# A new order of steps and PSUM banks in a two-attention, eight-expert layer

## The chip, the cores and the metric

One core of a Trainium2 chip runs the kernel. The metric is device microseconds of one execution. A core has TensorE (matmuls and transposes, with a weight load before each), VectorE, ScalarE, GpSimd, and SyncE, which only issues transfers. Each works through its own instructions in order and waits on semaphores. TensorE writes into eight PSUM banks; a bank holds 128 partitions of 512 floats.

## The reference, cut to what matters

```python
def _attn(q_in, k_in, v_in, wq, bq, wk, bk, wv, bv, wo, bo, causal):
    Q = (q_in @ wq + bq).reshape(Bq, Sq, H, HD)       # H = 16 heads of HD = 8
    Kp = (k_in @ wk + bk).reshape(Bq, Sk, H, HD)
    V = (v_in @ wv + bv).reshape(Bq, Sk, H, HD)
    scores = einsum('bqhd,bkhd->bhqk', Q, Kp) / sqrt(HD)     # causal mask in the first
    return einsum('bhqk,bkhd->bqhd', softmax(scores), V).reshape(Bq, Sq, Dm) @ wo + bo

def _moe(x, rw, rb, w1, b1, w2, b2):                  # E = 8 experts, K = 2 of them per token
    router_weights = softmax(xf @ rw + rb)
    topw, topi = top_k(router_weights, K);  topw = softmax(topw)
    h = gelu(einsum('td,edf->etf', xf, w1) + b1)      # D = 128, F = 512
    eo = einsum('etf,efd->etd', h, w2) + b2
    return einsum('etd,te->td', eo, combine)

x = _layernorm(x + _attn(x, x, x, ..., True), ln1_g, ln1_b)
x = _layernorm(x + _attn(x, ctx, ctx, ..., False), ln2_g, ln2_b)
x = _layernorm(x + _moe(x, ...), ln3_g, ln3_b)
```

x is 16 sequences of 128 tokens of 128 floats, the context 16 sequences of 77 tokens. All in float32.

## The kernel before, in words

The 16 sequences are worked on in eight pairs, p = 0 to 7. Each pair goes through self-attention (`SA`), cross-attention (`CA`) and routing (`RT`). Each of these is cut into named steps: `turn` (transpose the input), `project` and `project_keys`, `spread_terms` and `spread_keys` (lay the 16 heads out over the partitions), `values`, `scores` in four parts, `shift` (the negative row maxima, transposed and added to the queries as extra rows), `weights` in four parts (scores again and exp), `mix` in four parts (weights times values), `restore` in four parts (transpose back and divide), `turn_heads` and `norm` (output projection, residual, layer norm). Parts 0 and 1 are of sequence u = 0 of the pair, parts 2 and 3 of u = 1. In `scores` and `weights` a part covers two groups of heads, one in each of the two banks that the step has.

Two copies are made by transfers: `spread_keys` writes ku by VectorE, and SyncE copies it into km, from which `scores` reads; `spread_terms` writes qu by ScalarE, and SyncE copies it into qm. Both are issued at u = 1 (lines 469 and 482).

Routing: `route` (transpose and logits; ScalarE copies r_xT between them), `gate`, `choose`, `second` (two top-1 searches of small VectorE operations), `place` (rank in each expert's region by matmul), `number` (row numbers, then GpSimd's four indirect transfers of the pair's token rows into the DRAM array `dispatched`, line 1259). Before a pair's rows are sent, its share of `dispatched` has to be filled with a neutral row: `fill`, two transfers by SyncE (line 455). Each waits for the dispatch of the pair before it (line 452), and `number` waits for the fill (line 1253).

Experts (`MOE`): 39 tiles of 128 rows, `slots`. The first 17 can be settled after pair 5 (`count`, `table`), the rest after pair 7. `rows` n loads tile n from `dispatched` (line 511), `slot_turn` transposes it and VectorE copies it and the expert's first-layer weights into place (lines 1156, 1157), `slot_hidden` does the first layer and gelu, `slot_output` the second layer, and GpSimd scatters the result (line 1264). The weights of both layers, 2 MB each, lie where SA's large buffers were, so `first_layer` (line 498) waits for SA's last scores and `second_layer` (line 503) for its last weights. The first load waits for the table and for pair 5's dispatch:

```python
    if n == 0:
        sp.wait_ge(s_table, EARLY_OPS)
        sp.wait_ge(r.s_disp, KNOWN * 4 * 16)
        sp.wait_ge(SA.s_u_ps, PAIRS * 4)
        sp.wait_ge(SA.s_t_ps, PAIRS * 4)
```

and VectorE's first `slot_turn` waits for the first layer's weights (line 1150, `dve.wait_ge(s_w1, 16)`).

The order of all steps is one list written out. `ORDER` holds (kind, step, part, ahead); `iteration(i)` runs it with pair i + ahead, for i = -1 to 6, and each engine takes from it the steps in which it has work, in that order. Then `FINAL`, with explicit pairs, does what is left. So the order on each engine is the list, filtered: a step moved in the list moves on all engines that have a part in it, and on no other.

`home` gives each step its bank or banks; `last_home` holds for pair 7. On TensorE, `take(b)` waits until the last user of bank b has been read out, which is what `give(b, semaphore, value)` noted. A step that takes a bank right behind another waits for the engine that reads that bank.

After the tail of slots, the results are loaded back in four parts, summed, normed and stored.

## Time and profile before

| | us |
|---|---|
| median of the timed runs (463.62 to 465.36) | 464.87 |
| the profiled execution | 461.8 |
| its span | 460.1 |

The page begins with the busy time of each engine. A timeline row says when an instruction started (us from the span's start), how long it took, engine, line, what it wrote and read, and in brackets how long the engine was idle before it and what ended that. `bank` is PSUM; sa_, ca_ and r_ are tiles of the two attentions and the router. PEld is TensorE's weight load, SPq SyncE's queue; there the length is the time of issuing, not of the transfer. sa_over_km and sa_over_qm are the two layers' weights, sa_pt<-dispatched a load of expert rows. The granted clock is the share of full speed that TensorE had.

### The profile page before, as it was taken

The numbers are of one execution on the slowest core, as the hardware profiler recorded it, in microseconds if no ns is written. First come the engines' busy times: TensorE is split into PE (matmuls) and PEld (weight loads), VectorE is DVE, ScalarE is ACT, GpSimd is POOL, SyncE is SP. The second block draws the span as 40 slices with busy tenths as digits, with TensorE's granted clock in tenths as the row PEclk, the third lists the DMA queues.
The fourth block names the chain that finished last, engine by engine and source line by source line (L and its number), as shares of the span: only waits on it lengthen the run. The fifth ranks groups of instructions, "written<-read, shape, count | busy, mean of one in ns | idle before, by whom it ended". The sixth has DMA issues, their size and how long they took to land.

```text
span 460.1 us, 8844 instructions
## 1 busy us (share of the span) xinstructions
PE 367.9 (80%) x2122; PEld 245.3 (53%) x2122; DVE 310.2 (67%) x1075; ACT 293.0 (64%) x664; POOL 162.0 (35%) x212
## 2 busy tenths in 40 slices
PE   4388689988998998998988998889788578999600
PEld 2235355554564554645545545438656467999500
DVE  6153545678777787777877888876665774556366
ACT  4047249769768867967866966786795733555314
POOL 8312122132243144142253234241225254455522
PEclk9999879999999999999999999899999979999955
DMA  8700330621342333225036044682504113220063
GB/s 209 216 0 1 88 73 1 175 55 25 83 145 54 71 108 99 51 82 147 11 94 168 6 93 138 177 249 65 162 24 147 29 40 90 59 63 29 14 182 91
DMA packets 36073, 41.59 MB, mean 90 GB/s; under 512 B 4794, under 2 KB 28207, under 8 KB 36024
## 3 DMA queue, kind: packets, MB, share of 16 engines
q1 hardware_dynamic: 33752, 36.79, 30.4%
q0 software_dynamic: 2272, 4.24, 2.9%
q8 instruction: 20, 0.33, 0.3%
q14 instruction: 29, 0.24, 0.2%
HBM read 13.66 MB, written 14.79 MB: 62 GB/s over the span
## 4 chain that ended last, share of the span: by engine, by line
PE 49%; DVE 22%; issue 9%; ACT 8%; DMA 5%; POOL 4%; SPq 2%; DVEq 1%; POOLq 0%; ACTq 0%
PE bank L666 8%; PE bank L761 8%; PE bank L748 7%; PE bank L653 4%; ACT sa_qm L831 4%; DMA sa_km<-sa_ku 3%; PE bank L598 3%; PE bank L634 3%; DVE ca_nm L971 3%; PE bank L599 3%; PE bank L633 3%; PE bank L677 3%; POOL dispatched L1259 2%; SPq L469 2%; PE bank L641 1%
## 5 line engine op out<-in xcount | busy, mean ns | idle before, releaser
L890 ACT ACTIVATE sa_us<-bank,expert_b 128x128 f32<-128x128 f32 x156 | 44.4, 368 | 36.7 <-PE bank L748 30.9
L1236 POOL TENSOR_SCALAR_AFFINE_SELECT sa_pt<-sa_pt 128x512 f32<-128x512 f32 x64 | 39.0, 636 | 70.2 <-ACT sa_pt L839 69.9
L1264 POOL DMA_INDIRECT results<-sa_us,sa_pt x39 | 41.0, 1050 | 59.8 <-DVE sa_us L1169 44.6
L971 DVE TENSOR_REDUCE sa_nm<-bank 128x4 f32<-128x512 f32 x64 | 41.7, 685 | 18.9 <-PE bank L634 18.7
L761 PE MATMUL bank<-sa_over_qm,sa_us 128*128 x312 | 44.7, 289 | 5.7 <-DVE yb L1167 3.2
L831 ACT CAST sa_qm<-bank 8x512 fp32r<-8x512 f32 x64 | 36.8, 575 | 15.4 <-PE bank L641 14.1
L761 PEld LDWEIGHTS bank<-sa_over_qm,sa_us 128*128 128x128 f32 x312 | 39.8, 200 | 9.1 <-issue 8.9
L748 PE MATMUL bank<-xsT,sa_pt 128*128 128x128 f32 x312 | 43.2, 283 | 1.3 <-DVE sa_pt L1157 1.0
L839 ACT ACTIVATE sa_pt<-bank 128x512 f32<-128x512 f32 x64 | 34.8, 596 | 11.6 <-PE bank L653 11.5
L748 PEld LDWEIGHTS bank<-xsT,sa_pt 128*128 128x128 f32 x312 | 38.7, 195 | 4.2 <-DVE xsT L1156 2.2
L831 ACT CAST ca_qm<-bank 8x512 fp32r<-8x512 f32 x64 | 36.8, 575 | 5.2 <-PE bank L641 4.0
L634 PE MATMUL bank<-sa_km,sa_qu 128*128 128x512 f32 x64 | 39.4, 669 | 0.0
L1259 POOL DMA_INDIRECT dispatched<-r_sent,r_row x32 | 31.4, 981 | 21.2 <-issue 10.5
L839 ACT ACTIVATE ca_pt<-bank 77x512 f32<-77x512 f32 x64 | 33.8, 597 | 6.6 <-PE bank L653 6.6
L633 PE MATMUL bank<-causal_bf,ident_bf 128*128 128x512 bf16 x64 | 28.3, 442 | 11.9 <-DMA sa_km<-sa_ku 11.3
L666 PE MATMUL bank<-ca_pt,ca_vo 77*64 77x512 f32 x128 | 34.9, 617 | 1.1 <-DVE ca_lk L931 0.6
L666 PE MATMUL bank<-sa_pt,sa_vo 128*64 128x512 f32 x128 | 35.2, 632 | 0.0
L1244 POOL TENSOR_TENSOR sa_rs<-sa_ba,half 128x1 f32<-128x1 f32 x16 | 10.2, 634 | 68.4 <-DVE sa_ba L1015 68.4
L971 DVE TENSOR_REDUCE ca_nm<-bank 128x4 f32<-128x308 f32 x64 | 27.3, 472 | 7.3 <-PE bank L634 6.8
L653 PE MATMUL bank<-sa_qm,sa_ku 128*128 128x512 f32 x64 | 26.1, 482 | 5.7 <-ACT ca_qu L820 3.5
L846 ACT COPY ca_us<-bank 128x512 f32<-128x512 f32 x32 | 18.6, 589 | 15.0 <-PE bank L666 14.9
L633 PEld LDWEIGHTS bank<-causal_bf,ident_bf 128*128 128x128 bf16 x64 | 6.7, 105 | 36.7 <-DMA sa_km<-sa_ku 16.8
(218 smaller groups left out, 845.9 us busy)
## 6 DMA issues: line engine op xcount, KB each, us to landing
dispatched<-filler SPq DMA_DIRECT2D x17, 520.0 KB, 4.7
sa_km<-sa_ku SPq DMA_DIRECT2D x32, 128.0 KB, 2.4
sa_qm<-sa_qu SPq DMA_DIRECT2D x32, 96.0 KB
ca_qm<-ca_qu SPq DMA_DIRECT2D x32, 96.0 KB
sa_pt<-dispatched SPq DMA_DIRECT2D x39, 65.0 KB, 2.1
ca_km<-ca_ku SPq DMA_DIRECT2D x32, 77.0 KB, 2.1
sa_over_km<-in_e_w SPq DMA_DIRECT2D x1, 2048.0 KB, 9.1
sa_pt<-results SPq DMA_DIRECT2D x8, 256.0 KB, 4.8
```

The lines of the kernel that those rows point to most:

```text
L633: pe.matmul(dst, ident_bf[:, :], causal_bf[:, :].rearrange("q (o n) -> q o n", o=1).to_broadcast([P, J, P]), start=True, stop=False)
L634: pe.matmul(dst, k.qu[:, g, P * u:P * u + P], k.km[:, :, (2 * g + u) * k.keys:(2 * g + u) * k.keys + k.kpad], start=not k.causal, stop=Tru ...
L653: pe.matmul(bank[b][0:k.keys, :], k.ku[:, g, k.keys * u:k.keys * u + k.keys], k.qm[:, :, g, P * u:P * u + P], start=True, stop=True).then_ ...
L666: ins = pe.matmul(bank[b][64 * (g % 2):64 * (g % 2) + 64, :], k.vo[:, u, g, :], k.pt[u][:, 512 * g:512 * g + 512], start=True, stop=True)
L748: ins = pe.matmul(bank[b][:, P * (c if n < EARLY else c % 2):][:, 0:P], w1_now[n % 2][:, P * c:P * c + P], xsT[n % 2][:, :], start=True, s ...
L761: ins = pe.matmul(bank[b][:, 0:D], hid[n % 2][:, c, :], w2[:, bass.ds(expert, 1), c, :].rearrange("f o d -> f (o d)"), start=(c == 0), sto ...
L831: act.copy(k.qm[rows, j, :, P * u:P * u + P], src).then_inc(k.s_sha, 1)
L839: act.activation(k.pt[u][:, 512 * g:512 * g + 512], bank[home_of(p)[k, "weights", u][g % 2]][0:k.keys, :], ACT.Exp, scale=SCALE).then_inc( ...
L890: act.activation(hid[n % 2][:, c, :], bank[b][:, P * (c if n < EARLY else c % 2):][:, 0:P], ACT.Gelu, bias=b1[:, bass.ds(expert * FC + c, ...
L971: dve.tensor_reduce(k.nm[:, u, g, :], bank[home_of(p)[k, "scores", u][g % 2]][:, :].rearrange("q (j n) -> q j n", j=J)[:, :, 0:k.keys], AX ...
L1259: pool.indirect_dma_start(out=dispatched, out_offset=bass.IndirectOffsetOnAxis(ap=r.row[:, v, c:c + 1], axis=0), in_=r.sent[:, v, c, :], i ...
L1264: pool.indirect_dma_start(out=results, out_offset=bass.IndirectOffsetOnAxis(ap=xs[n % RING][:, P:P + 1].bitcast(I32), axis=0), in_=ys[n % ...
```

## The change

Only the three tables change: `ORDER` and `FINAL`, and the banks in `home` and `last_home`. Every engine does the same steps with the same operations as before. The head of `ORDER` is cut at another point (CA restore 2 and 3, project and project_keys now open the iteration), and within it steps trade places. `fill` was (RT, "fill", 0, -1) near the end, in front of (CA, "fetch", 0, 1); it is now (RT, "fill", 0, -2) near the head. SyncE takes part in SA turn, fetch, fill and the spread steps alone. In `FINAL`, `first_layer` comes behind rows 0, 1 and 2; before, it came in front of `second_layer` and all rows.

```diff
         ORDER = [
-            (SA, "scores", 2, 0), (CA, "turn_heads", 1, -2), (CA, "spread_terms", 0, -1), (CA, "spread_keys", 0, -1),
-            (CA, "spread_keys", 1, -1), (CA, "spread_terms", 1, -1), (CA, "norm", 1, -2), (SA, "weights", 0, 0),
-            (SA, "scores", 3, 0), (SA, "weights", 1, 0), (CA, "values", 0, -1), (RT, "route", 0, -2),
-            (RT, "gate", 0, -2), (SA, "mix", 0, 0), (SA, "shift", 1, 0), (CA, "scores", 0, -1),
-            (RT, "choose", 0, -2), (SA, "restore", 0, 0), (SA, "mix", 1, 0), (CA, "scores", 1, -1),
-            (SA, "weights", 2, 0), (CA, "scores", 2, -1), (SA, "turn", 0, 1), (SA, "weights", 3, 0),
-            (CA, "shift", 0, -1), (RT, "second", 0, -2), (CA, "scores", 3, -1), (SA, "restore", 1, 0),
-            (SA, "project", 0, 1), (SA, "project_keys", 0, 1), (SA, "mix", 2, 0), (CA, "weights", 0, -1),
-            (SA, "mix", 3, 0), (SA, "turn_heads", 0, 0), (CA, "shift", 1, -1), (RT, "place", 0, -2),
-            (SA, "spread_terms", 0, 1), (SA, "spread_keys", 0, 1), (SA, "restore", 2, 0), (SA, "spread_keys", 1, 1),
-            (SA, "spread_terms", 1, 1), (SA, "restore", 3, 0), (SA, "norm", 0, 0), (SA, "values", 0, 1),
-            (CA, "mix", 0, -1), (SA, "turn_heads", 1, 0), (CA, "weights", 1, -1), (SA, "norm", 1, 0),
-            (CA, "weights", 2, -1), (RT, "number", 0, -2), (CA, "restore", 0, -1), (CA, "mix", 1, -1),
-            (SA, "scores", 0, 1), (CA, "weights", 3, -1), (CA, "restore", 1, -1), (CA, "mix", 2, -1),
-            (SA, "scores", 1, 1), (CA, "turn_heads", 0, -1), (CA, "turn", 0, 0), (CA, "turn_context", 0, 0),
-            (RT, "fill", 0, -1), (CA, "mix", 3, -1), (SA, "shift", 0, 1), (CA, "norm", 0, -1),
-            (CA, "restore", 2, -1), (CA, "restore", 3, -1), (CA, "project", 0, 0), (CA, "project_keys", 0, 0),
-            (CA, "fetch", 0, 1)]
+            (CA, "restore", 2, -2), (SA, "values", 0, 0), (CA, "restore", 3, -2), (CA, "project", 0, -1),
+            (CA, "project_keys", 0, -1), (SA, "scores", 2, 0), (CA, "turn_heads", 1, -2), (RT, "fill", 0, -2),
+            (CA, "spread_terms", 0, -1), (CA, "spread_keys", 0, -1), (CA, "spread_keys", 1, -1),
+            (CA, "spread_terms", 1, -1), (CA, "norm", 1, -2), (SA, "weights", 0, 0), (SA, "scores", 3, 0),
+            (SA, "weights", 1, 0), (RT, "route", 0, -2), (SA, "mix", 0, 0), (RT, "gate", 0, -2), (SA, "shift", 1, 0),
+            (RT, "choose", 0, -2), (CA, "values", 0, -1), (SA, "restore", 0, 0), (SA, "mix", 1, 0),
+            (CA, "scores", 0, -1), (SA, "weights", 2, 0), (CA, "scores", 1, -1), (SA, "turn", 0, 1),
+            (SA, "weights", 3, 0), (CA, "shift", 0, -1), (RT, "second", 0, -2), (CA, "scores", 2, -1),
+            (SA, "restore", 1, 0), (SA, "mix", 2, 0), (CA, "scores", 3, -1), (SA, "project", 0, 1),
+            (SA, "project_keys", 0, 1), (CA, "weights", 0, -1), (SA, "turn_heads", 0, 0), (SA, "mix", 3, 0),
+            (SA, "spread_terms", 0, 1), (CA, "shift", 1, -1), (RT, "place", 0, -2), (SA, "spread_keys", 0, 1),
+            (SA, "spread_keys", 1, 1), (SA, "spread_terms", 1, 1), (SA, "restore", 2, 0), (SA, "restore", 3, 0),
+            (SA, "norm", 0, 0), (CA, "mix", 0, -1), (SA, "turn_heads", 1, 0), (CA, "weights", 1, -1),
+            (SA, "norm", 1, 0), (CA, "weights", 2, -1), (CA, "fetch", 0, 1), (RT, "number", 0, -2),
+            (CA, "mix", 1, -1), (CA, "mix", 2, -1), (CA, "restore", 0, -1), (SA, "scores", 0, 1),
+            (CA, "weights", 3, -1), (CA, "restore", 1, -1), (SA, "scores", 1, 1), (CA, "turn", 0, 0),
+            (CA, "turn_heads", 0, -1), (CA, "mix", 3, -1), (CA, "turn_context", 0, 0), (SA, "shift", 0, 1),
+            (CA, "norm", 0, -1)]
...
         home = {
-            (CA, "mix", 0): (6, 3), (CA, "mix", 1): (5, 2), (CA, "norm", 0): (5,), (CA, "norm", 1): (1,),
-            (CA, "project", 0): (0,), (CA, "project_keys", 0): (3,), (CA, "scores", 0): (2, 3),
-            (CA, "scores", 1): (6, 0), (CA, "shift", 0): (3,), (CA, "shift", 1): (7,), (CA, "spread_keys", 0): (6,),
-            (CA, "spread_keys", 1): (0,), (CA, "spread_terms", 0): (4,), (CA, "spread_terms", 1): (3,),
-            (CA, "turn", 0): (6,), (CA, "turn_context", 0): (7,), (CA, "turn_heads", 0): (4,),
-            (CA, "turn_heads", 1): (5,), (CA, "values", 0): (4,), (CA, "weights", 0): (3, 0),
-            (CA, "weights", 1): (7, 4), (RT, "place", 0): (2,), (RT, "route", 0): (5, 1), (SA, "mix", 0): (0, 1),
-            (SA, "mix", 1): (5, 4), (SA, "norm", 0): (1,), (SA, "norm", 1): (1,), (SA, "project", 0): (2,),
-            (SA, "project_keys", 0): (7,), (SA, "scores", 0): (0, 1), (SA, "scores", 1): (1, 7),
-            (SA, "shift", 0): (4,), (SA, "shift", 1): (5,), (SA, "spread_keys", 0): (1,),
-            (SA, "spread_keys", 1): (6,), (SA, "spread_terms", 0): (3,), (SA, "spread_terms", 1): (0,),
-            (SA, "turn", 0): (5,), (SA, "turn_heads", 0): (6,), (SA, "turn_heads", 1): (4,), (SA, "values", 0): (5,),
-            (SA, "weights", 0): (3, 2), (SA, "weights", 1): (4, 7)}
+            (CA, "mix", 0): (6, 3), (CA, "mix", 1): (5, 1), (CA, "norm", 0): (1,), (CA, "norm", 1): (5,),
+            (CA, "project", 0): (0,), (CA, "project_keys", 0): (3,), (CA, "scores", 0): (5, 2),
+            (CA, "scores", 1): (4, 0), (CA, "shift", 0): (3,), (CA, "shift", 1): (7,), (CA, "spread_keys", 0): (2,),
+            (CA, "spread_keys", 1): (7,), (CA, "spread_terms", 0): (4,), (CA, "spread_terms", 1): (4,),
+            (CA, "turn", 0): (5,), (CA, "turn_context", 0): (3,), (CA, "turn_heads", 0): (4,),
+            (CA, "turn_heads", 1): (1,), (CA, "values", 0): (1,), (CA, "weights", 0): (3, 5),
+            (CA, "weights", 1): (1, 6), (RT, "place", 0): (2,), (RT, "route", 0): (1, 4), (SA, "mix", 0): (2, 7),
+            (SA, "mix", 1): (5, 4), (SA, "norm", 0): (0,), (SA, "norm", 1): (7,), (SA, "project", 0): (1,),
+            (SA, "project_keys", 0): (6,), (SA, "scores", 0): (2, 0), (SA, "scores", 1): (5, 6),
+            (SA, "shift", 0): (7,), (SA, "shift", 1): (6,), (SA, "spread_keys", 0): (0,),
+            (SA, "spread_keys", 1): (6,), (SA, "spread_terms", 0): (3,), (SA, "spread_terms", 1): (1,),
+            (SA, "turn", 0): (7,), (SA, "turn_heads", 0): (2,), (SA, "turn_heads", 1): (4,), (SA, "values", 0): (4,),
+            (SA, "weights", 0): (3, 0), (SA, "weights", 1): (4, 1)}
...
         FINAL = [
...
-            (SA, "shift", 1, 7), (RT, "second", 0, 5), (SA, "restore", 0, 7), (MOE, "first_layer", 0, 0),
-            (CA, "scores", 0, 6), (CA, "turn_context", 0, 7), (CA, "scores", 1, 6), (MOE, "second_layer", 0, 0),
...
-            (SA, "turn_heads", 0, 7), (CA, "weights", 0, 6), (CA, "shift", 1, 6), (MOE, "table", 0, 0),
-            (CA, "mix", 0, 6), (SA, "restore", 2, 7), (MOE, "rows", 0, 0), (SA, "restore", 3, 7),
-            (CA, "weights", 1, 6), (SA, "norm", 0, 7), (SA, "turn_heads", 1, 7), (CA, "project_keys", 0, 7),
-            (MOE, "rows", 0, 1), (CA, "restore", 0, 6), (SA, "norm", 1, 7), (MOE, "rows", 0, 2),
-            (CA, "weights", 2, 6), (MOE, "rows", 0, 3), (MOE, "rows", 0, 4), (CA, "mix", 1, 6),
-            (CA, "weights", 3, 6), (CA, "mix", 2, 6), (CA, "turn", 0, 7), (CA, "restore", 1, 6), (MOE, "rows", 0, 5),
-            (CA, "spread_keys", 0, 7), (CA, "spread_keys", 1, 7), (MOE, "slot_turn", 0, 0), (CA, "turn_heads", 0, 6),
-            (CA, "project", 0, 7), (CA, "norm", 0, 6), (CA, "mix", 3, 6), (MOE, "slot_hidden", 0, 0),
-            (MOE, "slot_turn", 0, 1), (CA, "values", 0, 7), (CA, "restore", 2, 6), (CA, "restore", 3, 6),
-            (MOE, "slot_turn", 0, 2), (MOE, "slot_hidden", 0, 1), (MOE, "slot_output", 0, 0),
...
+            (SA, "weights", 3, 7), (CA, "shift", 0, 6), (RT, "number", 0, 5), (CA, "scores", 2, 6),
+            (SA, "mix", 2, 7), (CA, "scores", 3, 6), (CA, "weights", 0, 6), (MOE, "count", 0, 0), (SA, "mix", 3, 7),
+            (CA, "shift", 1, 6), (SA, "turn_heads", 0, 7), (MOE, "table", 0, 0), (SA, "restore", 2, 7),
+            (CA, "mix", 0, 6), (MOE, "second_layer", 0, 0), (SA, "restore", 3, 7), (MOE, "rows", 0, 0),
+            (CA, "weights", 1, 6), (CA, "restore", 0, 6), (SA, "turn_heads", 1, 7), (CA, "project_keys", 0, 7),
+            (CA, "weights", 2, 6), (SA, "norm", 0, 7), (SA, "norm", 1, 7), (MOE, "rows", 0, 1), (MOE, "rows", 0, 2),
+            (MOE, "first_layer", 0, 0), (CA, "mix", 1, 6), (MOE, "rows", 0, 3), (CA, "mix", 2, 6),
+            (CA, "weights", 3, 6), (CA, "spread_keys", 0, 7), (CA, "restore", 1, 6), (CA, "turn", 0, 7),
+            (CA, "spread_keys", 1, 7), (MOE, "slot_turn", 0, 0), (CA, "project", 0, 7), (CA, "restore", 2, 6),
+            (CA, "mix", 3, 6), (MOE, "slot_turn", 0, 1), (CA, "turn_heads", 0, 6), (MOE, "rows", 0, 4),
+            (MOE, "slot_hidden", 0, 0), (CA, "norm", 0, 6), (CA, "spread_terms", 0, 7), (MOE, "slot_turn", 0, 2),
+            (MOE, "slot_hidden", 0, 1), (CA, "restore", 3, 6), (MOE, "slot_output", 0, 0), (MOE, "rows", 0, 5),
...
```

The lines of `FINAL` left out interleave the steps of pairs 6 and 7 with slots 0 to 16 in nearly the order of before, and `last_home` gets other banks throughout.

## Rows read from the trace of the kernel before

**Rows 1.** The page: busy time of each engine, its share of the span, instructions.
```profile
PE 367.9 (80%) x2122; PEld 245.3 (53%) x2122; DVE 310.2 (67%) x1075; ACT 293.0 (64%) x664; POOL 162.0 (35%) x212
```

**Rows 2.** Windows of three stages: length, PE, PEld, DVE, ACT, POOL busy, clock, DMA, GB/s.
```profile
171.70:208.60 36.90, 33.49 (x184) 19.86 (x182) 28.83 (x102) 28.19 (x59) 12.63 (x20) 1.00 0.35 94
284.20:360.00 75.80, 62.88 (x385) 42.83 (x385) 53.54 (x210) 55.62 (x124) 26.60 (x36) 0.98 0.46 131
360.00:431.00 71.00, 61.97 (x489) 58.16 (x488) 43.11 (x157) 37.63 (x120) 33.59 (x32) 0.95 0.18 50
```

**Rows 3.** Timeline, TensorE, one iteration: start, length, ..., [idle before, released by].
```profile
172.42 0.70 PE L653 MATMUL bank<-sa_qm,sa_ku 128*128 128x512 f32 x2 [0.55 <-ACT ca_qu L820]
175.71 0.61 PE L706 MATMUL bank<-router_w,r_xT 128*128 128x8 f32 x4 [0.49 <-ACT r_xT L858]
183.45 0.33 PE L641 MATMUL bank<-cst,ca_mm 128*128 128x128 f32 x1 [1.00 <-DVE ca_mm L981]
199.71 0.39 PE L633 MATMUL bank<-causal_bf,ident_bf 128*128 128x512 bf16 x1 [0.41 <-DVE sa_nm L971]
203.31 1.09 PE L677 MATMUL bank<-cst,ca_us 128*128 128x128 f32 x8 [0.38 <-DVE ca_y L1009]
206.38 0.39 PE L598 MATMUL bank<-ca_hq,spread_hq 128*128 128x256 f32 x1 [0.25 <-DVE ca_lq L931]
```

**Rows 4.** Timeline, SyncE's queue, the same iteration.
```profile
205.17 0.94 SPq L455 DMA_DIRECT2D dispatched<-filler  x2
206.15 1.07 SPq L428 DMA_DIRECT2D ca_cin<-in_ctx  x1
208.63 2.46 SPq L469 DMA_DIRECT2D ca_km<-ca_ku  x4
```

**Rows 5.** The page's DMA issues: bytes of one, median us from issue to landing.
```profile
dispatched<-filler SPq DMA_DIRECT2D x17, 520.0 KB, 4.7
sa_over_km<-in_e_w SPq DMA_DIRECT2D x1, 2048.0 KB, 9.1
```

**Rows 6.** A source line, timeline rows of the same iteration, two groups of the page.
```profile
L962 DVE TENSOR_TENSOR sa_vo<-bank,sa_rows x8: 416/417/426, 14.2 to 267.9; 128x256 f32<-128x256 f32 x8
...
183.32 0.16 DVE L1071 SCALAR_TENSOR_TENSOR r_by_expert<-r_by_expert 128x16 f32<-128x16 f32 x1
185.07 0.16 DVE L1076 TENSOR_TENSOR r_by_token<-r_by_token 128x2 f32<-128x2 f32 x1
...
196.29 0.10 PEld L633 LDWEIGHTS bank<-causal_bf,ident_bf 128*128 128x128 bf16 x1 [0.81 <-DMA sa_km<-sa_ku]
...
L971 DVE TENSOR_REDUCE ca_nm<-bank 128x4 f32<-128x308 f32 x64 | 27.3, 472 | 7.3 <-PE bank L634 6.8
L846 ACT COPY ca_us<-bank 128x512 f32<-128x512 f32 x32 | 18.6, 589 | 15.0 <-PE bank L666 14.9
```

**Rows 7.** Timeline, SyncE's queue, at the first expert tile.
```profile
292.37 0.52 SPq L498 DMA_DIRECT2D sa_over_km<-in_e_w  x1
296.23 0.82 SPq L503 DMA_DIRECT2D sa_over_qm<-in_e_w  x1
310.19 6.32 SPq L511 DMA_DIRECT2D sa_pt<-dispatched  x6
```

**Rows 8.** Timeline, GpSimd's dispatch of pair 5, and landing of all 32 such transfers.
```profile
302.51 0.96 POOL L1259 DMA_INDIRECT dispatched<-r_sent,r_row  x1 [0.31 <-issue]
...
DMA to landing us min/median/max: 2.3/2.3/7.2
```

**Rows 9.** Windows of 2 us around the weight loads, columns as in rows 2.
```profile
292.00:294.00 2.00, 2.00 (x6) 0.91 (x7) 1.79 (x7) 1.35 (x3) 0.40 (x1) 0.56 0.60 135
296.00:298.00 2.00, 2.00 (x13) 0.99 (x11) 1.79 (x7) 1.98 (x4) 1.22 (x2) 1.00 1.03 393
306.00:308.00 2.00, 1.48 (x11) 1.00 (x10) 1.40 (x6) 1.37 (x4) 1.05 (x2) 1.00 0.92 283
```

**Rows 10.** Timeline, VectorE's copy in the first slot_turn.
```profile
313.54 0.29 DVE L1156 COPY xsT<-bank 128x128 f32<-128x128 f32 x1 [0.52 <-issue]
```

More of the change, by code:

```diff
@@ L378, in build @@
-        last_home = {**home,
-            (CA, "mix", 0): (5, 2), (CA, "mix", 1): (5, 1), (CA, "norm", 0): (2,), (CA, "norm", 1): (1,),
-            (CA, "scores", 0): (5, 6), (CA, "scores", 1): (1, 0), (CA, "shift", 0): (2,), (CA, "shift", 1): (4,),
-            (CA, "spread_keys", 0): (2,), (CA, "spread_keys", 1): (7,), (CA, "spread_terms", 0): (2,),
-            (CA, "spread_terms", 1): (2,), (CA, "turn_heads", 0): (6,), (CA, "turn_heads", 1): (1,),
-            (CA, "values", 0): (1,), (CA, "weights", 0): (6, 7), (CA, "weights", 1): (3, 1), (RT, "place", 0): (6,),
-            (RT, "route", 0): (4, 5)}
+            (CA, "restore", 2, -2), (SA, "values", 0, 0), (CA, "restore", 3, -2), (CA, "project", 0, -1),
@@ new lines, in build @@
+        last_home = {**home,
+            (CA, "mix", 0): (0, 2), (CA, "mix", 1): (1, 5), (CA, "norm", 0): (2,), (CA, "norm", 1): (3,),
+            (CA, "scores", 0): (6, 5), (CA, "scores", 1): (7, 0), (CA, "shift", 0): (1,), (CA, "shift", 1): (5,),
+            (CA, "spread_keys", 0): (2,), (CA, "spread_keys", 1): (2,), (CA, "spread_terms", 0): (2,),
+            (CA, "spread_terms", 1): (4,), (CA, "turn_heads", 0): (3,), (CA, "turn_heads", 1): (0,),
+            (CA, "values", 0): (3,), (CA, "weights", 0): (1, 4), (CA, "weights", 1): (3, 5), (RT, "place", 0): (5,),
+            (RT, "route", 0): (0, 2)}
```

67 lines of the change are left out of this document (34 added, 33 removed).

## The prediction

> **What bounds the kernel now.** I read the page's busy shares first: TensorE 80%, VectorE 67%, ScalarE 64% [rows 1]. An average over stages with different limits says little, so the next view was the busy time by stage [rows 2]. In a steady iteration (36.9 us from one to the next; five of them, pairs 2 to 6) TensorE is busy 33.5 us, VectorE 28.8, ScalarE 28.2: TensorE bounds it, and a new order can at most give back the time in which TensorE waits. In the last attention part and the first expert tiles (284 to 360 us) TensorE has 62.9 of 75.8 us, in the rest of the expert tiles 62.0 of 71 [rows 2]. So three views follow: TensorE's own rows with their waits in one iteration, SyncE's queue there, and the same two around the first expert tile.
>
> TensorE's rows that have idle time in front of them in one iteration are six: 0.55, 0.49, 1.00, 0.41, 0.38 and 0.25 us, together 3.08 us [rows 3]. That is the most that the change can win per iteration, 15.4 us over five. SyncE waits for the dispatch of the pair before, issues the two fills at 205.17, the context load at 206.15 and the km copies of CA at 208.63 [rows 4]. None of the six waits names a DMA.
>
> **The filler.** From the two lists, SyncE's program before is: SA copies, fill, fetch, then CA copies. After it is: SA copies, fetch, fill, then CA copies. `fill` moves to the head of the next iteration with its pair lowered by one, so it is the same fill, with the same wait for the same dispatch. Only the 77 KB context load steps in front of it. It was needed some 30 us later (the turn of the context follows in the next iteration), so it wins nothing: 0 us. The CA copies still stand behind the filler: the chain and TensorE's waits [rows 3] show no one waiting for them now, and CA's first scores move later in the order, so that stays hidden; if it were not, the price would be a copy that lands behind a fill, which takes 4.7 us [rows 5]; an iteration would lose at most that.
>
> **The steady iteration, edit by edit.** (a) SA weights 0 took bank 3 right behind CA spread_terms 1, and so waited 0.55 us for ScalarE's copy. It now takes 3 and 0, which the two CA projections left long before: -0.55. The route after it is then held by ScalarE (exp of weights 1, then r_xT), so the 0.49 there stays and the 0.55 is kept. (b) CA norm 0 and CA restore 2 shared bank 5; they now have 1 and 5: -0.38. (c) SA values moves from before CA mix 0 to between CA restore 2 and 3. TensorE's part is the same work. VectorE's 0.42 us [rows 6] now stands in front of ca_lq, for which TensorE already waits (0.25): +0.25. (d) CA scores 2 goes behind CA shift 0: two reductions of 0.47 us [rows 6] leave VectorE's path to ca_mm, values' 0.42 us enters it: at most -0.5 of the 1.00. But ScalarE now does SA mix 0's copy (0.59) [rows 6] in front of the gate's exp, for which VectorE's `choose` waits, and CA scores 0 takes bank 2 from SA restore 0: +0.6. (e) CA scores 3 takes banks 4 and 0 again behind scores 2, and VectorE has `second` in front of their reductions, nine operations from 183.32 to 185.23, 1.9 us [rows 6]. By these rows ca_mm ends at 182.9, `second` at 184.8, both reductions at 185.8; TensorE comes there at 185.2 with shift, scores 2, restore 1, mix 2 and half of scores 3 behind it: 12 matmuls at this iteration's mean of 33.49 / 184 = 0.18 us, 2.2 us [rows 2]: +0.5. (f) CA mix 2 is pulled in front of SA scores 0, where a weight load waited 0.81 us for the km copy [rows 6]; matmuls in flight covered most of it: -0.3. The 0.41 us at SA scores 1 shrinks, since number and both norms end earlier on VectorE: -0.3. Sum: -0.55 - 0.38 + 0.25 - 0.5 + 0.6 + 0.5 - 0.3 - 0.3 = -0.68; one iteration's rounding apart, I take -0.6. Bounds: -3.08 (all six waits gone) and +0.5 (of the gains only (a) holds, of the losses none is covered: -0.55 + 0.25 + 0.6 + 0.5 = +0.8, less the 0.3 of (f)). Five iterations: -3.0, from -15 to +2.5; the start, bound by copies and casts, 0, between -1 and +1.
>
> **The first expert tile.** Here the change moves a load that matters. Before, SyncE issues the first layer's weights (2 MB) at 292.37, the second layer's at 296.23, and the first six loads of expert rows from 310.19 [rows 7]. After, the order is second layer, rows 0, 1, 2, first layer, rows 3. Rows 0 waits for the dispatch of pair 5. Its last indirect transfer is issued from 302.51 to 303.46, and such transfers land 2.3 us later in the median, 7.2 at most [rows 8]; the maximum falls in the window in which both weight loads fill the DMA engines (393 GB/s at 296 us, still 283 at 306) [rows 9]. With only the second layer in flight at 296, its 2 MB are through by about 304 (2,048 KB at 283 GB/s are 7.4 us), so rows 0 goes at 303.46 + 2.3 = 305.8, say 306; with no gain it stays 310.2. Three row loads take 6.32 / 6 x 3 = 3.2 us, so the first layer goes at 309.2. It took 9.1 us [rows 5]; 2,048 KB at 393 GB/s are 5.3. Nearest is the 9.1, which was shared from 296 on; I take 8: landing at 317.2, between 306 + 3.2 + 5.3 = 314.5 and 310.2 + 3.2 + 9.1 = 322.5.
>
> VectorE waits for it in slot_turn 0, whose copy ran at 313.54 [rows 10]. Its work up to there is the same in both orders. So it stands still from 313.5 to 317.2: +3.6, between +1.0 and +9.0. Behind it in VectorE's queue are ca_lq of the last pair, restore 2, slot_turn 1 and CA norm 0; TensorE can still do project, restore 2 and mix 3, then stops at slot_turn 1 for the bank, and hidden 0 (a microsecond behind that copy before) goes at about 318. Nothing later has slack of that size for all engines at once, so it passes through. The clock comes on top: before, after TensorE stood idle around 290 us its granted clock was 0.56 in the next 2 us slice [rows 9], which is the 1.2 GHz level for nearly all of it. If the new stall does the same for 4 us, 2 us of work are added; one case in three to me: +0.6.
>
> The Trainium skill bears on the dispatch. Its page "DMA: Bandwidth & Descriptors", section "Queues, rings and completion order", says that each DMA engine takes turns between the queues it has work for. By that rule the dispatch, on another queue than the weights, would not stand behind them. The trace does not fit it simply: 7.2 us against 2.3. If the dispatch is slow beside any weight load, rows 0 goes at up to 310 and the stall is 7 us or more; that is the second rival.
>
> The rest of the last list (fill 6 and 7, rows 4 to 16, slots) keeps SyncE's sequence but for single swaps; slots 9 to 16 beside pair 7's routing trade places by one step each. No row tells a sign: 0, between -2 and +2.
>
> **Sum.** The profiled execution took 461.8 us (span 460.1). 461.8 - 3.0 + 3.6 + 0.6 + 0 = 463.0. The median of the timed runs is 464.87, 3.07 above the profiled one, so the forecast is 466.0, 0.2% above before: no change that shows. About 0.5% (2.3 us) is what a measurement of this kernel can tell from none.
>
> **Rivals.** First, faster: the banks and the pulled mix 2 win 1.5 us per iteration, half of rows 3, and the first layer lands in 5.3 us: -7.5 + 1.0 + 0 = -6.5, 458.4. For it: three of the six waits are bank waits that the new homes remove by construction. Against: VectorE's unbroken work from `choose` to ca_lq. Second, slower: the load of the first layer, put behind rows 2, becomes the wait that ends last: +7 in slot_turn 0 and +1 of clock, with -3.0 in the iterations: 469.9. It decides as soon as the load lands after 315.8, where its stall reaches the 2.3 us that can be told, if the iterations give nothing. Third, the change does not do what it says: the filler's place in the queue is the same, the six waits are traded among engines (0), and only the +4.2 stays: 469.1.
>
> **How the numbers follow.** Forecast (gain and stall about cancel) 0.40, faster rival 0.26, second rival 0.20, third 0.14. The forecast's own range, 463 to 468.5, lies mostly within 462.6 to 467.2; of its 0.40, 0.33 is "same", 0.05 slower, 0.02 faster. Faster 0.28, same 0.36 (with 0.03 from the rivals' near ends), slower 0.36. The range takes in both sides: 458.5 to 471.
>
> **What would show it.** Period between equal steps in the iterations: 36.3 us; at 36.9 or above the steady part is wrong. The bank wait before SA weights 0 gone, a new wait before CA scores 3 for ca_nm. SyncE: rows 0 at about 306 and the first layer about 3 us behind (less what was won before); VectorE idle before slot_turn 0 for 3 to 4 us, released by the DMA of sa_over_km. If that wait is under 1 us, or if an iteration wins more than 1.5 us, the forecast is wrong on the side of faster; if the stall is above 6 us, slower.

## The result

| | us, median | runs |
|---|---|---|
| before | 464.25 | 4 |
| after | 479.38 | 4 |

The ratio is 1.0347 (95% interval 1.0301 to 1.0392): slower by 3.5%, outside my range. The profiled execution of after took 480.33 us, its span is 478.6. Line numbers of after are those of before plus one, as the repeated order is one line longer.

The page's busy times, then the windows of one iteration, of the stretch from pair 6's CA key copies through the first expert tiles, and of the rest up to the loads of the results, answer to [rows 1, 2]; the columns are the same.

```profile
PE 374.7 (78%) x2122; PEld 254.4 (53%) x2122; DVE 313.9 (66%) x1075; ACT 295.3 (62%) x664; POOL 162.3 (34%) x212
```
```profile
167.28:204.85 37.57, 33.74 (x185) 20.39 (x184) 29.50 (x102) 28.52 (x59) 12.78 (x20) 1.00 0.33 85
281.68:360.00 78.32, 54.59 (x300) 37.48 (x301) 45.80 (x183) 49.21 (x104) 22.63 (x30) 0.90 0.43 122
360.00:455.26 95.26, 79.97 (x583) 73.00 (x579) 51.78 (x188) 44.86 (x140) 40.82 (x41) 0.88 0.15 41
```

An iteration is a little longer. From 281.7 to 360 us TensorE has 54.6 us of work in 78.3, where it had 62.9 in 75.8 [rows 2], and the granted clock of both later windows is down. TensorE's waits in one iteration, for [rows 3]:

```profile
170.63 0.61 PE L707 MATMUL bank<-router_w,r_xT 128*128 128x8 f32 x4 [0.70 <-ACT r_xT L859]
172.66 0.33 PE L642 MATMUL bank<-cst,sa_mm 128*128 128x128 f32 x1 [0.41 <-DVE sa_mm L982]
175.53 0.41 PE L635 MATMUL bank<-ca_km,ca_qu 128*128 128x312 f32 x1 [0.32 <-DVE sa_on L998]
178.85 0.33 PE L642 MATMUL bank<-cst,ca_mm 128*128 128x128 f32 x1 [1.00 <-DVE ca_mm L982]
181.20 0.80 PE L635 MATMUL bank<-ca_km,ca_qu 128*128 128x312 f32 x2 [0.28 <-DVE ca_nm L972]
198.48 0.46 PE L691 MATMUL bank<-ca_square,ca_oT 128*128 128x128 f32 x2 [0.29 <-issue]
201.52 0.39 PE L634 MATMUL bank<-causal_bf,ident_bf 128*128 128x512 bf16 x1 [0.57 <-DVE ca_on L998]
```

They sum to 3.57 us against 3.08. SyncE's queue in the iteration, and at the first expert tile, for [rows 4, 7]:

```profile
201.01 0.94 SPq L456 DMA_DIRECT2D dispatched<-filler  x2
204.85 2.46 SPq L470 DMA_DIRECT2D ca_km<-ca_ku  x4
...
292.54 0.82 SPq L504 DMA_DIRECT2D sa_over_qm<-in_e_w  x1
305.56 3.04 SPq L512 DMA_DIRECT2D sa_pt<-dispatched  x3
308.65 0.43 SPq L499 DMA_DIRECT2D sa_over_km<-in_e_w  x1
```

The load of the first layer's weights (w1, `sa_over_km`; those of the second layer are w2, `sa_over_qm`) leaves after rows 0 to 2, and the page's DMA issues, for [rows 5], have it landing 10.3 us later:

```profile
dispatched<-filler SPq DMA_DIRECT2D x17, 520.0 KB, 4.4
...
sa_over_km<-in_e_w SPq DMA_DIRECT2D x1, 2048.0 KB, 10.3
```

The timelines of VectorE and TensorE show who waits for it, for [rows 10]. A second stall stands 38 us further on; what ended it the trace calls only "remote":

```profile
319.93 0.29 DVE L1157 COPY xsT<-bank 128x128 f32<-128x128 f32 x1 [9.35 <-DMA sa_over_km<-in_e_w]
357.88 0.29 DVE L1157 COPY xsT<-bank 128x128 f32<-128x128 f32 x1 [4.39 <-remote]
```
```profile
320.37 0.45 PE L739 MATMUL bank<-cst,sa_pt 128*128 128x128 f32 x1 [8.31 <-DVE xsT L1157]
358.31 0.45 PE L739 MATMUL bank<-cst,sa_pt 128*128 128x128 f32 x1 [3.09 <-DVE xsT L1157]
```

### The profile page after: what moved, and what is told of

Its sections match the earlier page's. It is cut to its first block, busy times and chain, and to the rows that moved or that the text cites. A ratio compares the mean times of both kernels' runs of the same rounds, so it can differ in the third digit from the quotient of the medians.

```text
span 478.6 us, 8836 instructions
## 1 busy us (share of the span) xinstructions
PE 374.7 (78%) x2122; PEld 254.4 (53%) x2122; DVE 313.9 (66%) x1075; ACT 295.3 (62%) x664; POOL 162.3 (34%) x212
## 4 chain that ended last, share of the span: by engine, by line
PE 46%; DVE 22%; issue 11%; POOL 6%; DMA 6%; ACT 4%; SPq 2%; DVEq 1%; another core or an unknown queue 1%; POOLq 0%; ACTq 0%
PE bank L749 7%; PE bank L667 7%; PE bank L762 7%; PE bank L635 4%; POOL dispatched L1260 4%; PE bank L599 4%; PE bank L654 3%; PE bank L600 3%; PE bank L634 3%; DMA sa_over_km<-in_e_w 2%; DVE ca_nm L972 2%; PE bank L678 2%; PE bank L691 2%; ACT sa_qm L832 2%; POOL ca_rs L1245 1%
## 5 line engine op out<-in xcount | busy, mean ns | idle before, releaser
L749 PE MATMUL bank<-xsT,sa_pt 128*128 128x128 f32 x312 | 49.9, 311 | 2.7 <-DVE sa_pt L1158 1.0
L749 PEld LDWEIGHTS bank<-xsT,sa_pt 128*128 128x128 f32 x312 | 45.0, 222 | 6.8 <-issue 3.4
L762 PEld LDWEIGHTS bank<-sa_over_qm,sa_us 128*128 128x128 f32 x312 | 41.0, 205 | 8.6 <-issue 8.4
L635 PE MATMUL bank<-sa_km,sa_qu 128*128 128x512 f32 x64 | 37.6, 645 | 0.0
L634 PE MATMUL bank<-causal_bf,ident_bf 128*128 128x512 bf16 x64 | 27.0, 423 | 11.3 <-DMA sa_km<-sa_ku 8.6
L1157 DVE COPY xsT<-bank 128x128 f32<-128x128 f32 x39 | 11.4, 292 | 35.6 <-PE bank L749 9.7
L1245 POOL TENSOR_TENSOR ca_rs<-ca_ba,half 128x1 f32<-128x1 f32 x16 | 9.8, 610 | 50.8 <-DVE ca_ba L1016 49.9
## 6 DMA issues: line engine op xcount, KB each, us to landing
sa_over_km<-in_e_w SPq DMA_DIRECT2D x1, 2048.0 KB, 10.3
```

Of the source, the lines that this page charges most:

```text
L634: pe.matmul(dst, ident_bf[:, :], causal_bf[:, :].rearrange("q (o n) -> q o n", o=1).to_broadcast([P, J, P]), start=True, stop=False)
L635: pe.matmul(dst, k.qu[:, g, P * u:P * u + P], k.km[:, :, (2 * g + u) * k.keys:(2 * g + u) * k.keys + k.kpad], start=not k.causal, stop=Tru ...
L749: ins = pe.matmul(bank[b][:, P * (c if n < EARLY else c % 2):][:, 0:P], w1_now[n % 2][:, P * c:P * c + P], xsT[n % 2][:, :], start=True, s ...
L762: ins = pe.matmul(bank[b][:, 0:D], hid[n % 2][:, c, :], w2[:, bass.ds(expert, 1), c, :].rearrange("f o d -> f (o d)"), start=(c == 0), sto ...
```

## The experiments

Four theories: A, the late load of w1 is the loss; B, the new last list is slow by itself; C, the repeated order is; and E, the filler's place. D, F and G are named where they come up. All ratios are to the kernel before beside them on one chip, 95% intervals in brackets. Experiments 1 and 2 ran on one chip, 3, 4 and 5 and the run of bank 5 in 7 on a second, the others on a third; the kernel before took 459.2, 460 to 461 and 463 to 464 us there.

**1. The load alone, put back and put late.** In after (edit of the last list; `+` where it stands now, `-` where it stood):

```
 (SA, "restore", 0, 7),
+(MOE, "first_layer", 0, 0),
 ...
 (MOE, "rows", 0, 2),
-(MOE, "first_layer", 0, 0),
```

> The changed kernel with one step put back: the load of the first layer stands again behind restore 0 of the last pair, in front of second_layer, and no longer behind rows 2. Theory A (the late load of w1 is the loss): the 9.35 us that VectorE waits in front of slot_turn 0 go, and with them the 8.3 us of TensorE and about 2 us of the lower clock behind them: 469 us (467 to 471). The second stall at 354 to 358 us stays. Rival B (the new order of the last list is slow by itself, and the w1 wait only takes slack from it): no more than 3 us come back, 476 to 479 us, and other waits of TensorE grow between 320 and 355 us.

Measured 463.03 us, 1.0121 [1.0071, 1.0171]: 4 us below the range of theory A, so more came back than the stall and the clock that it counted, though after itself was not run on this chip. No wait for the load is left in its trace, and no second stall either, which A had staying. In before, the opposite edit:

```
 (CA, "turn_context", 0, 7), (CA, "scores", 1, 6),
-(MOE, "first_layer", 0, 0),
 ...
 (MOE, "rows", 0, 2),
+(MOE, "first_layer", 0, 0),
```

> The kernel before with one step moved: first_layer stands behind rows 2 instead of in front of second_layer; nothing else differs. Rows 2 leaves SyncE at about 311 to 313 us, so w1 lands at about 322. Theory A: VectorE waits some 8 us before slot_turn 0 (313.5 us before), and the run takes 472 us (470 to 475). Rival B (only the whole new order loses, this load is hidden by other work): 464 to 467 us.

Measured 469.90 us, 1.0253 [1.0197, 1.0309], 10.7 us over before, just below A's range (470 to 475). SyncE's row and VectorE's:

```profile
307.87 0.43 SPq L498 DMA_DIRECT2D sa_over_km<-in_e_w  x1
```
```profile
318.40 0.29 DVE L1156 COPY xsT<-bank 128x128 f32<-128x128 f32 x1 [9.42 <-DMA sa_over_km<-in_e_w]
```

The same stall in a kernel in which nothing else is new. A stands in both directions, B falls.

**2. The two halves of the change crossed.** Repeated order and homes of one kernel, last list and homes of the other; the six steps in which they overlap are dropped or put in front:

```
FINAL = [(RT, "fill", 0, 5), (CA, "restore", 2, 5), (CA, "restore", 3, 5), (SA, "values", 0, 7),
         (CA, "project_keys", 0, 6), (CA, "project", 0, 6), <the last list of before>]
```

> The repeated order and its PSUM homes are those of before, the last list and its homes those of after (without its first six steps, which the repeated order of before has already done). Theory A (the loss lies in the last list): about 480 us (478 to 484), the small head start of the new loop (2.5 us at the last pair) lost too. Rival C (the loss comes from the new repeated order, by the state in which it hands over): 470 us or less.

> The repeated order and its homes are those of after, the last list and its homes those of before, with the six steps in front that the new repeated order leaves to it. Theory A: 462 us (459 to 465), the new loop's head start of 2.5 us kept. My prediction's steady term (-0.6 us an iteration) would give the same 461; but the trace after shows a period of 37.6 us against 36.9, so a head start early on of over 5 us should shrink to 2 or 3 us at the last pair. Rival C: 470 us or more.

Measured 481.02 us, 1.0526 [1.0462, 1.0590], and 478.05 us, 1.0431 [1.0379, 1.0483]. The second looks like C, but is not: its repeated part keeps the period of after (37.4 to 37.7 us from one CA key copy to the next), and the step over the join (from pair 5's CA key copies to pair 6's) takes 47.9 us, where after has 39.3; the other cross takes 46.6 where before has 38.4. The stretch behind it, to the first tile's copy, is 38.1 us long in the second cross (290.28 to 328.41), with no wait for w1, where the run with the early load in experiment 1 has 29.6. So a join costs 8 to 9 us in one step, and here as much again behind it; that banks and steps of the two lists don't fit each other is my reading, not shown. Theory A's 462 us for this cross was missed by 16 us, and the experiment can't separate the halves. C is decided by experiment 3.

**3. Where the load may stand, and the references on one chip.** In after, `first_layer` directly in front of rows 0, three steps of SyncE earlier:

```
 (SA, "restore", 3, 7),
+(MOE, "first_layer", 0, 0),
 (MOE, "rows", 0, 0),
```

> The changed kernel with first_layer moved only three steps forward on SyncE: it stands directly in front of rows 0 (behind second_layer) instead of behind rows 2. Theory A (w1 comes after what VectorE has ready): SyncE issues w1 next to w2, at 293 to 294 us instead of 308.65, since nothing between them has to be waited for but rows 0 itself; it lands at 303 to 304, before VectorE asks for it at 310.6, and the run is as fast as with the load 21 us earlier: 463 us (461 to 466). Rival D (w1 and w2 together slow the scattered writes of pair 5, and rows 0 with them): rows 0 leaves 2 us or more later, 467 to 470 us.

> The changed kernel itself, beside the others on one chip. Expected 3.0 to 3.9% over before. The stall of VectorE of 4.39 us at 354 to 358 us, which ends on nothing that the kernel waits for by its own program, should come again in its trace if it belongs to the kernel; theory A needs only the first one (9.35 us before slot_turn 0) to be there.

> The kernel before itself, for a trace of it on the same chip as the others. Expected no difference, and steady periods of 36.6 to 37.1 us against 37.4 to 37.6 of the changed kernel.

Measured: 459.88 us, 1.0002 [0.9973, 1.0031]; after 473.05, 1.0285 [1.0251, 1.0319]; before 460.81, 1.0012 [0.9988, 1.0036]. Three steps of one queue are 13 us. C falls too: this kernel has the new repeated order and takes as long as before. Rows 0 left 2.3 us later than in after on the same chip (309.01 against 306.68), as rival D said, but it cost no time. (In the traces before is 4.0 us shorter than the kernel with the load in front of rows 0, with spans of 455.7 and 459.7; their medians don't show that difference.) I had the landing at 303 to 304; it was issued at 295.08 behind w2, and took 16.0 us to 311.1, just in time. SyncE's queue, then the landing of that load, then VectorE:

```profile
294.22 0.82 SPq L504 DMA_DIRECT2D sa_over_qm<-in_e_w  x1
295.08 5.39 SPq L499 DMA_DIRECT2D sa_over_km<-in_e_w  x1
309.01 3.03 SPq L512 DMA_DIRECT2D sa_pt<-dispatched  x3
```
```profile
DMA to landing us min/median/max: 16.0/16.0/16.0
```
```profile
313.47 0.29 DVE L1157 COPY xsT<-bank 128x128 f32<-128x128 f32 x1 [0.52 <-issue]
```

These two traces, of one chip and without the second stall, are compared to see where 13 us come from when TensorE's wait is 7.3 (VectorE's is 8.3). Windows between equal steps: pair 6's CA key copies, first tile's copy, row loads behind fill 7, next row loads, loads of the results. With the load in front of rows 0:

```profile
283.37:313.47 30.10, 24.30 (x122) 13.06 (x123) 22.95 (x91) 21.50 (x44) 10.92 (x16) 0.94 0.60 180
313.47:349.10 35.63, 29.86 (x188) 22.37 (x189) 22.67 (x92) 28.11 (x63) 11.74 (x14) 0.95 0.37 98
349.10:378.59 29.49, 20.88 (x152) 18.50 (x150) 20.47 (x87) 15.37 (x40) 11.59 (x14) 0.94 0.20 55
378.59:436.25 57.66, 50.98 (x423) 48.10 (x423) 31.55 (x102) 28.39 (x100) 29.42 (x28) 0.98 0.19 52
```

The changed kernel:

```profile
283.01:320.41 37.40, 24.89 (x124) 13.19 (x123) 22.87 (x91) 22.25 (x45) 10.93 (x16) 0.90 0.58 159
320.41:358.23 37.82, 31.47 (x176) 24.82 (x178) 22.96 (x92) 26.25 (x58) 11.72 (x14) 0.83 0.29 79
358.23:389.28 31.05, 23.26 (x153) 20.06 (x150) 19.93 (x86) 16.80 (x43) 11.14 (x13) 0.84 0.19 52
389.28:448.17 58.89, 51.98 (x432) 48.87 (x431) 31.71 (x102) 28.58 (x100) 29.91 (x28) 0.98 0.19 51
```

The stall makes the first stretch 7.3 us longer. The other three have the same work between them (763 and 761 matmuls) and are 5.0 us longer together, as is TensorE's busy time. Is all of that the price of the stall? The 6 us from the first tile's copy on, with the early load and then in the changed kernel:

```profile
313.47:319.47 6.00, 5.59 (x42) 4.44 (x43) 4.60 (x17) 4.35 (x13) 0.84 (x2) 1.00 0.40 90
320.41:326.41 6.00, 5.49 (x25) 5.17 (x26) 3.52 (x13) 2.92 (x7) 0.84 (x2) 0.50 0.00 1
```

Behind the stall the granted clock is 0.50, the 1.2 GHz level, for these 6 us, and 0.99 in the next 6. From the first tile's copy to the router's matmul that follows it took 12.7 us (320.41 to 333.10), with the early load 10.6 (313.47 to 324.06):

```profile
324.06 0.61 PE L707 MATMUL bank<-router_w,r_xT 128*128 128x8 f32 x4 [0.46 <-ACT r_xT L859]
333.10 0.61 PE L707 MATMUL bank<-router_w,r_xT 128*128 128x8 f32 x4 [0.46 <-ACT r_xT L859]
```

So 2.1 us are the clock right behind the stall. The other 2.9 come later, the last 1.2 of them at the same clock of 0.98, and they are not shown to follow from it: the new order with an early load and without a second stall took 122.8, 123.7 and 126.6 us in three traces from the first tile's copy to the loads of the results, with 101.7, 102.6 and 106.5 us of TensorE; the changed kernel here took 127.8, with 106.7. What else makes the 13 us of the medians stays open.

**4. The filler alone.** In before, `fill` moves behind `turn_heads` 1 of the next iteration, and so behind the fetch of the context. It still stands in front of the CA key copies, as it does in the changed kernel; the text below says otherwise, and is wrong there:

```
 (CA, "turn_heads", 1, -2),
+(RT, "fill", 0, -2),
 ...
-(RT, "fill", 0, -1),
```

> The kernel before with nothing changed but the place of fill: in every iteration it stands one step behind turn_heads 1 of the next one, so that the fetch of the context and the CA key copies leave SyncE in front of the filler's two transfers, as they do in the changed kernel. My prediction: worth nothing, since the fetched context is used an iteration later and the key copies land in time; 0 +- 1 us against before. Rival E (the filler in front delays the key copies and these the scores): 1 to 5 us faster, the period of 36.9 us shorter.

Measured 460.05 us, 0.9975 [0.9941, 1.0009], with periods of 37.2, 36.6, 36.9, 36.6 where before in the same set has 37.2, 36.2, 36.9, 36.6. SyncE's queue in it:

```profile
196.33 0.33 SPq L427 DMA_DIRECT2D ca_cin<-in_ctx  x1
200.12 0.94 SPq L454 DMA_DIRECT2D dispatched<-filler  x2
```

Its key copies follow at 203.52. The filler's new place is worth nothing, and E falls as an account of the change. What key copies in front of the filler would give was not run.

**5. VectorE's order around the stall, and the place of the load once more.**

```
-(CA, "spread_keys", 1, 7), (MOE, "slot_turn", 0, 0), (CA, "project", 0, 7), ...
+(CA, "spread_keys", 1, 7), (CA, "project", 0, 7), ..., (CA, "spread_terms", 0, 7),
+(MOE, "slot_turn", 0, 0), (MOE, "slot_turn", 0, 1), (MOE, "slot_hidden", 0, 0), ...
```

> The changed kernel with the load of w1 left where it is (behind rows 2), but slot_turn 0, slot_turn 1 and slot_hidden 0 moved behind spread_terms 0 of pair 7 in the last list, so that VectorE and TensorE do project 7, restore 2, mix 3, turn_heads 0 and norm 0 of pairs 6 and 7 first. Theory A (the stall is the distance between w1's landing at 319 to 320 us and VectorE's turn to copy the first tile; everything behind it in VectorE's own order waits too): some 3 us of VectorE's work go in front, the wait before slot_turn 0 shrinks from 8 or 9 us to 5 or 6, and the run is 2.5 to 4 us faster than the changed kernel: 1.020 to 1.024 of before where the changed kernel had 1.0285. Rival F (the expert tiles' own chain sets the end, and w1's landing alone starts it): no gain, 1.027 to 1.030.

Measured 472.28 us, 1.0242 [1.0197, 1.0287], beside 1.0285 of after in its own set. The two engines' rows:

```profile
320.50 0.29 DVE L1157 COPY xsT<-bank 128x128 f32<-128x128 f32 x1 [4.54 <-DMA sa_over_km<-in_e_w]
```
```profile
320.94 0.45 PE L739 MATMUL bank<-cst,sa_pt 128*128 128x128 f32 x1 [6.34 <-DVE xsT L1157]
```

VectorE's wait fell by 3.8 us, TensorE's only from 7.3 to 6.3, and from pair 6's key copies to the results it took 164.8 us where after took 165.2. The ratio is just above A's range (1.020 to 1.024) and below F's (1.027 to 1.030), and its interval reaches into both, so the times don't decide; the trace is nearer to rival F.

> The changed kernel with first_layer behind restore 0 of the last pair, 7 us earlier than directly in front of rows 0. It took 1.0121 of before on one chip, while the load in front of rows 0 took 1.0002 on another. If the place of the load makes this difference, 1.010 to 1.014 again here; if it was the chip and the runs of the kernel before beside it, 1.000 to 1.008.

Measured 462.58 us, 1.0047 [1.0007, 1.0086]; so the 1.0121 of experiment 1 was partly its set. With three ratios of 1.0002, 1.0047 and 1.0121, the new order with an early load is up to 1.2% slower than before, and in no set faster.

In before, `first_layer` directly in front of rows 0:

> The kernel before with first_layer directly in front of rows 0, behind the load of w2, instead of in front of w2. Theory A: w1 lands before VectorE asks for it at 313.5 us, so nothing is lost: within 0.5% of before. Rival: the transfer stands beside rows 0 and the scattered writes and holds them up, 2 us or more.

Measured 459.35 us, 0.9966 [0.9920, 1.0012]: as expected, free.

**6. How the loss grows with the landing.** The load in two halves, waited for together; and the load behind rows 4.

```
+half = slice(EXPERTS // 2 * n, EXPERTS // 2 * n + EXPERTS // 2)
-sp.dma_start(w1, moe["w1"].rearrange("e d f -> d e f")).then_inc(s_w1, 16)
+sp.dma_start(w1[:, half, :], moe["w1"][half].rearrange("e d f -> d e f")).then_inc(s_w1, 16)
 ...
-dve.wait_ge(s_w1, 16)
+dve.wait_ge(s_w1, 32)
```

> The changed kernel itself, as the reference of this set: 1.026 to 1.035 of before; w1 issued at about 309, landed at about 319.5, VectorE's wait before slot_turn 0 8 to 9.5 us.

> The changed kernel with the load of w1 in two halves: experts 4 to 7 behind restore 0 of the last pair, experts 0 to 3 where the whole load stands now (behind rows 2); slot_turn 0 waits for both. The late half issues at 309 and lands in some 5 to 6 us, at about 315, so the wait is 3.5 to 4.5 us instead of 8 to 9. If the loss is proportional to the landing (13 us for 8.3), the run takes 1.012 to 1.016 of before; if any stall there has a fixed price of some 5 us, 1.020 or more; if the first microseconds are covered by other work, 1.008 or less.

> The changed kernel with first_layer moved from behind rows 2 to behind rows 4 on SyncE: issued at about 315.5, landing at about 325.5, a wait of 14 to 15 us. Proportional 1.6 to 1: the loss against the load in front of rows 0 grows by 9 to 10 us, 1.047 to 1.052 of before; one to one behind a fixed price: by 6 us, 1.040 to 1.044; less than that if work not bound to w1 moves into the gap.

| on one chip | wait before slot_turn 0 | us | ratio |
|---|---|---|---|
| half of w1 late | 3.8 | 475.27 | 1.0245 [1.0194, 1.0297] |
| after | 8.2 | 479.59 | 1.0350 [1.0299, 1.0400] |
| behind rows 4 | 13.7 | 484.74 | 1.0440 [1.0386, 1.0493] |

The waits grow by 4.4 and 5.5 us, the medians by 4.3 and 5.1: one to one, on top of a fixed price, as one of the expectations had it each time. Less its own wait, each of the three is 8 us above the 463.29 of before. The clock is one part of it: with half of w1 late it was 0.72 in the 6 us behind the first tile's copy. The rows of VectorE (half late, then behind rows 4):

```profile
316.58 0.29 DVE L1159 COPY xsT<-bank 128x128 f32<-128x128 f32 x1 [3.77 <-DMA sa_over_km<-in_e_w]
```
```profile
324.25 0.29 DVE L1157 COPY xsT<-bank 128x128 f32<-128x128 f32 x1 [13.71 <-DMA sa_over_km<-in_e_w]
```

All three have the second stall (4.3 to 4.5 us). It may be a part of the fixed price here, but the kernel before was not traced on this chip, where even a variant of it has such a stall (the last section).

**7. The longer period.** After with the load in front of rows 0, and in the repeated order

```
 (SA, "weights", 1, 0),
+(CA, "values", 0, -1),
 (RT, "route", 0, -2),
 ...
-(CA, "values", 0, -1),
```

with bank 5 for it, then with bank 7, in place of 1.

> The changed kernel with first_layer in front of rows 0, and in the repeated order the step values of the cross-attention put back in front of route (its place in the kernel before), with PSUM bank 5 for it up to pair 6. The steady period was 37.4 to 37.6 us against 36.6 to 36.9 of before, and the trace has 0.70 us of TensorE's wait for r_xT in front of the router's matmul. Theory G (waits whose cover was moved away make the period longer): that wait shrinks to 0.2 us or less, the period to 37.0 to 37.2, the run by 2 us: 457 to 459 us. Rival: another wait takes its place, the period stays at 37.4 to 37.6.

> As the kernel in which values of the cross-attention stands in front of route again, but with PSUM bank 7 for it instead of 5, whose last holder (the copy of spread_keys 1) is done before. There the period was 38.3 to 38.9 us with a wait of 0.75 us for bank 5 (released by sa_nm) and 0.46 for r_xT. Theory G: with bank 7 the 0.75 goes and the period is 37.2 to 37.5, no longer than the 37.5 of the order of after. If the period stays at 38.3 or more, it is the order of the step and not its bank.

Measured 467.39 us, 1.0183 [1.0127, 1.0239], and 468.24 us, 1.0136 [1.0093, 1.0179]; periods 38.3 to 38.9, and 37.3 to 37.7. TensorE's rows with bank 5:

```profile
170.68 0.63 PE L618 MATMUL bank<-ca_square,ca_cT 128*77 128x128 f32 x4 [0.75 <-DVE sa_nm L972]
171.99 0.61 PE L707 MATMUL bank<-router_w,r_xT 128*128 128x8 f32 x4 [0.46 <-ACT r_xT L859]
```

and with bank 7:

```profile
170.62 0.61 PE L707 MATMUL bank<-router_w,r_xT 128*128 128x8 f32 x4 [0.55 <-ACT r_xT L859]
```

A wrong bank is worth 1 us per iteration. The cover for r_xT alone is worth nothing: with bank 7 its wait shrinks by 0.15, not to 0.2, and the period stays that of after, where theory G had first put 37.0 to 37.2. The run of bank 7 has the second stall as well (3.6 us).

**8. The two small differences together.** Experiment 4's edit and the load in front of rows 0, both in before.

> The kernel before with two edits: fill one step behind turn_heads 1 of the next iteration, and first_layer directly in front of rows 0. If both small differences are real, 0.992 to 0.996 of before; if they are noise, 0.998 to 1.002. The mean is 0.997, with nothing in the traces (periods 36.6 to 36.9 us in both) that would explain a gain: I expect no measurable difference.

Measured 463.44 us, 1.0009 [0.9975, 1.0043]. No version here beats the kernel before.

## Why the prediction was wrong

**The accounts.** From the two references of experiment 3, after against before: at the second CA key copies 1.8 us ahead (92.25 against 94.05), at pair 6's 3.7 behind (283.01 against 279.31), from there to the first tile's copy 9.1 longer (37.40 against 28.32), from there to the results 3.1 longer (127.76 against 124.67), and 0.4 shorter behind. 3.7 + 9.1 + 3.1 - 0.4 = 15.5, the difference of the spans 471.2 and 455.7. For the two traces of the forecast and of the result: 5.7 ahead at the second key copies, 3.2 longer to pair 6's, 8.9 to the first tile's copy (38.25 against 29.39), 12.0 to the results (135.33 against 123.33), 0.1 behind: 18.5, the difference of 478.6 and 460.1.

**The filler, 0:** right, shown by experiment 4 for the place that the change gives it.

**The steady iteration, -0.6:** wrong in sign; this step failed too. From the second CA key copies to pair 6's, five periods, nine traces with the new repeated order took 189.1 to 190.8 us, six with the old one 185.3 to 186.4: +0.8 each, about +3.8 where I had -3.0. The last of the five, over the join to the last list, is 38.4 before and 39.2 to 39.5 after. (a) and (b) came as put: the bank waits before SA weights 0 and CA restore's matmul (0.55, 0.38) are gone; so is the 0.25 for ca_lq that (c) had growing. Of (d) nothing was won, the 1.00 for ca_mm is the same to the hundredth. (e) cost 0.28, not 0.5. The 0.41 at SA scores 1 that (f) had shrinking is gone. The 0.32 for sa_on is the bank that (d) had CA scores 0 take from SA restore 0. What I had not named is 0.57 for ca_on in front of SA scores 2, which now takes bank 5 behind CA restore 2, and 0.41 for sa_mm, beside 0.21 more for r_xT and 0.29 of issue. I had counted gains where the waits stood, and not gone through every step of the new order for the bank that it takes and the work that had covered it. Which of the new order's steps makes the 0.8 is not settled; experiment 7 excludes the place of `values` alone.

**The start, 0:** nearly. The trace of before that stands above reached its second CA key copies at 97.78; its later one at 94.05. Most of the 5.7 us by which after was ahead there is a difference between executions of one kernel, not of the change; 1.8 are left.

**The first expert tile, +3.6: this step failed.** Its path was right: rows 0 at 306 (305.56), the load at 309.2 (308.65), VectorE's wait before slot_turn 0 released by it. Its size was not: 9.35 us, beyond the bound of 9.0. Pair 6 stood 2.5 us earlier in this trace (281.68 against 284.15), and with it VectorE (at 310.6, not 313.5) and GpSimd's last dispatch (300.06, not 302.51); that shift alone leaves the wait nearly as it was. Three terms were too small. From the end of that dispatch's issue to rows 0 I had 2.3 us, and it took 4.5 (301.02 to 305.56), so rows 0 was no earlier although the dispatch was. The landing of w1, 8 us by my choice between 5.3 and 9.1, took 10.3, with row loads and key copies beside it. And the copy began 1.0 us behind the landing (318.95, 319.93), for which I had nothing.

**The clock, +0.6:** the mechanism and the 2 us were right, the chance of one in three too low. Experiment 3 shows 2.1 us, at a clock of 0.50; in the first trace of after it was 0.68 in the 6 us behind the first tile's copy, and half a load late has it too.

**The rest of the last list, 0:** in the first trace of after there is the second stall of 4.39 us, which no step of mine had, and this stretch is 12.0 us longer there. It is not fixed to the change: the later trace of the same kernel doesn't have the stall, is 3.1 us longer than before in this stretch, and the ratio there is 1.0285 instead of 1.0347.

**The second rival** had the mechanism (it "becomes the wait that ends last"), with 7 and 1 where 8 to 9 and about 2 were measured, and -3.0 in the iterations where about +3.8 was. I gave it 0.20. Its own test, slower if the stall is above 6 us, decided rightly.

## What to carry to other kernels

Of a large load that is moved behind others in a queue, compare the worst landing with the earliest time at which its reader can come, and bound in the same way every transfer that it has to wait behind: this one was free three steps earlier and cost 13 us where it stood. To a stall of TensorE add what it does afterwards: here a stall of 7 us cost another 2 in slower matmuls right behind it. Before a longer tail is called the price of a stall, compare it with several traces that have no stall: they differed by 4 us. And a trade of waits between engines in a saturated loop is read from what each step covers and whose bank it takes, not only from the wait that its new place removes.
